# Building the one-hot matrix of an edge step with four VectorE comparisons instead of one

## What is computed

```python
Wh = (h @ W).reshape(N, HEADS, OUT_CH)                     # N = 6250, 4 heads x 64
e = einsum(Wh[edge_row], a_src) + einsum(Wh[edge_col], a_dst)
e = exp(leaky_relu(e) - max)
e_sum = segment_sum(e, edge_row)
alpha = e / (e_sum[edge_row] + 1e-15)
h_new = segment_sum(Wh[edge_col] * alpha, edge_row)        # a sum per target node
```

## Time and profile before

| | |
|---|---|
| median of 3 runs | 4566.98 us (4551.9 to 4567.17) |
| the profiled execution | 4563.81 us |
| its span, first to last instruction | 4561.9 us |
| busy: PE / DVE / ACT / POOL | 73% / 59% / 39% / 56% |
| stretch with the key side, 208 steps | 630 to 1939 us |
| stretch with the query side, 196 steps | 1939 to 3450 us |
| last stretch, 36 steps | 3450 to 3680 us |

### The profile page before, as it was taken

How to read it: one execution, slowest core, us unless ns; L and a number is a source line. 1 busy time by engine, 2 the same in 40 slices (tenths; PEclk the granted TensorE clock), 3 DMA queues, 4 the chain that set the end, 5 groups by cost and what they waited for, 6 DMA issues and landing times.

```text
span 4561.9 us, 90761 instructions
## 1 busy us (share of the span) xinstructions
PE 3309.0 (73%) x23188; PEld 2345.3 (51%) x23505; DVE 2688.7 (59%) x6015; ACT 1791.1 (39%) x4855; POOL 2546.9 (56%) x2454
## 2 busy tenths in 40 slices
PE   5888747767767777777777777777776545877895
PEld 2333324444444444456665666666564435665785
DVE  9888876657667666655555555555554463534222
ACT  3666422223323223244444444444443212543563
POOL 4566457767778867755565555555555613234223
PEclk8676668879989979889888989989897776988998
DMA  2222123333333323322222222222222232334344
GB/s 66 77 76 77 60 84 90 87 94 91 98 93 94 106 78 91 98 73 73 70 76 68 73 75 72 71 75 71 68 74 64 72 127 71 110 105 146 97 133 138
DMA packets 260611, 394.74 MB, mean 87 GB/s; under 512 B 71952, under 2 KB 195022, under 8 KB 260232
## 3 DMA queue, kind: packets, MB, share of 16 engines
q0 software_dynamic: 86704, 239.52, 18.9%
q1 hardware_dynamic: 150924, 132.95, 9.4%
q10 hardware_dynamic: 22860, 20.83, 1.6%
HBM read 308.82 MB, written 84.30 MB: 86 GB/s over the span
## 4 chain that ended last, share of the span: by engine, by line
PE 29%; issue 20%; DVE 13%; another core or an unknown queue 12%; DVEq 12%; ACT 7%; POOL 4%; ACTq 2%; DMA 1%; POOLq 0%; SPq 0%
PE bank L1935 6%; PE bank L1856 5%; DVEq L1445 4%; DVEq L1468 4%; PE bank L2123 3%; PE bank L2135 3%; DVEq L1444 3%; PE bank L1858 2%; PE bank L1969 2%; ACT away L1028 2%; DVE room L1438 1%; POOL room L805 1%; PE bank L1924 1%; DVE room L1464 1%
## 5 line engine op out<-in xcount | busy, mean ns | idle before, releaser
L805 POOL DMA_INDIRECT room<-table,room x1564 | 1804.0, 1153 | 1091.6 <-DVE room L1464 645.5
L1935 PE MATMUL bank<-room 128*128 128x260 f32 x3520 | 1020.7, 439 | 380.3 <-issue 208.0
L1935 PEld LDWEIGHTS bank<-room 128*128 128x128 f32 x3520 | 730.5, 218 | 512.0 <-issue 398.9
L1484 DVE TENSOR_TENSOR room<-room 128x1024 f32<-128x1024 f32 x392 | 481.2, 1228 | 533.0 <-issue 499.1
L1464 DVE TENSOR_TENSOR room<-room 128x1024 f32<-128x1024 f32 x440 | 537.0, 1220 | 389.7 <-ACT room L1037 268.4
L1028 ACT ACTIVATE away<-bank,minus_p 128x512 bf16<-128x512 f32 x440 | 301.7, 686 | 1084.7 <-remote 980.2
L1969 PE MATMUL bank<-ident,room 128*128 128x128 f32 x1764 | 262.1, 299 | 206.6 <-DVE room L1487 142.7
L1856 PE MATMUL bank<-room 128*128 128x264 f32 (+1 forms) x588 | 312.8, 673 | 65.8 <-issue 34.4
L1031 ACT ACTIVATE spare<-away,ones 128x512 bf16<-128x512 bf16 x440 | 317.6, 722 | 54.2
L1969 PEld LDWEIGHTS bank<-ident,room 128*128 128x128 f32 x1764 | 218.6, 154 | 197.1 <-issue 185.6
L1924 PE MATMUL bank<-rowt,spare 128*128 128x8 bf16 x7040 | 262.1, 167 | 73.2 <-issue 72.5
(11 more groups left out here) (313 smaller groups left out, 4793.0 us busy)
## 6 DMA issues: line engine op xcount, KB each, us to landing
room<-table,room POOLq DMA_INDIRECT x1564
kv_dram<-room SPq DMA_DIRECT2D x49, 324.0 KB, 2.2
room<-kv_dram SPq DMA_DIRECT2D x196, 81.0 KB
y_dram<-planes SPq DMA_DIRECT2D x119, 128.0 KB
room<-xs_dram ACTq DMA_DIRECT2D x110, 128.0 KB
q_dram<-room SPq DMA_DIRECT2D x49, 192.0 KB, 1.8
room<-q_dram SPq DMA_DIRECT2D x196, 48.0 KB
table<-room SPq DMA_DIRECT2D x49, 130.0 KB, 2.1
```

The lines of the kernel that those rows point to most:

```text
L805: pool.indirect_dma_start(G[:, k.slot, u, :], None, table, bass.IndirectOffsetOnAxis(ap=ixbuf[:, k.slot, u:u + 1].bitcast(I32), axis=0)).t ...
L1484: dve.tensor_tensor(f.rearrange("p h (d i) -> p h d i", i=MD), over(x, [[XD, 2], [0, h], [1, MD]]), over(x, [[XD, 2], [1, h], [1, MD]]), A ...
L1935: ins = pe.matmul(pbank[1 + h][:, 0:TW], OH[:, s, u, :], Gw[:, h, u, :], start=(u == 0), stop=(u == U - 1))
```

## The change

The one comparison of two inputs (`iota_f` repeated four times, and the four row numbers each repeated 128 times, 512 columns) becomes four comparisons of 128 columns, each with one row number per partition as a scalar operand. All four write their quarter of the same slot of `OH`; the semaphore is raised by the last.

```diff
             if k.after(4):
                 dve.wait_ge(agg_made, k.n - 3)
-            dve.tensor_tensor(OH[:, s, :, :], iota_f[:].unsqueeze(1).to_broadcast([P, U, P]),
-                              row_step[:, bass.ds(k.n, 1), :].rearrange("p a u -> p (a u)").unsqueeze(2).to_broadcast([P, U, P]),
-                              ALU.is_equal).then_inc(oh_done, 1)
+            for u in range(U):
+                ins = dve.tensor_scalar(OH[:, s, u, :], iota_f[:], row_step[:, bass.ds(k.n, 1), u:u + 1].rearrange("p a u -> p (a u)"), None, ALU.is_equal)
+            ins.then_inc(oh_done, 1)
```

## The result

| | before | after |
|---|---|---|
| median | 4559.44 us (4 runs, 4551.77 to 4567.17) | 4697.49 us (4 runs, 4687.35 to 4716.8) |
| the profiled execution's span | 4561.9 us | 4686.7 us |

The ratio is 1.0308, with a 95% interval from 1.0262 to 1.0353: the change costs 138 us. The forecast was 4650 us, 1.8% slower, so the sign and the mechanism came true and the sum of 88 us was 50 us too small. The two profiled executions lie 125 us apart; between them all of the misfit lies in the first stretch, as will be seen.

The account below looks back on a forecast made before the run. The prediction took VectorE's queue to bound the first stretch, and partly the second, with a TensorE-ScalarE circle. Terms 53 + 19 + 11 + 5 = 88 us gave 4652 from the profiled run, forecast as 4650 us; range 4575 to 4730 us.

Parts of the forecast that it names:

- The bound: VectorE's queue, handing over loads ahead of `features`, outlasts its datapath by 0.94 us in steps of the key side.
- The price of a pair: On VectorE's queue, one address computation with its instruction costs 0.15 us; three more cost 0.45 us per loop step.
- Who pays: Key side: three of four steps, less 18 waiting for ScalarE, pay 0.45 us each: 53 us.
- The knock-on: Steps where `weigh` waits for ScalarE were only taken off the paying ones: 18 on key side, 79 on query side.
- The second stretch: Query side: 38 us of queue delay, half counted because a later ScalarE wait may swallow it: 19 us.
- The last stretch: Last 32 loop steps: three of four pay 0.45 us of queue work, 11 us.
- The fixed-address steps: 40 steps outside loops: three bare instructions more, half of 0.24 us of comparison time counted each, 5 us.
- The datapath: VectorE's four comparisons take 0.84 us against 0.60; the 0.24 us more is hidden beside the queue in loop steps.
- GpSimd: Gathers waiting for `weigh` before reusing a place: nothing counted; at most 0.24 us in each of 440 steps, 106 us.
- Absorbed: Rival: TensorE, ScalarE and VectorE's circle sets the lap, ScalarE waits shrink; some 11 us, 4575 us, chance 0.15.
- Faster: Rival: comparisons cost 0.13 us each on the datapath, `weigh` ends 0.07 us earlier; at most 31 us gained, chance 0.05.
- Lock: Rival: each comparison waits 0.49 us for a GpSimd gather; 220 us, 4870 us; sign, comparisons over 0.5 us; chance 0.07.

Follow-up runs that it names:

- five increments: Kernel before, plus five increments of an idle semaphore on VectorE's queue behind the comparison of each loop step: 4211.51 us against 4081.43, ratio 1.0315.
- fixed-place kernel: Changed kernel, its four comparisons reading row numbers from fixed places, without address work: 4087.09 us against 4081.43 for the kernel before; on another chip 4475.7 against 4470.54.
- eight comparisons: Kernel with four comparisons reading fixed places, plus four more per loop step into a spare place: 4636.74 us against 4461.63 for the kernel before, ratio 1.0392.

## Why the prediction was right, and where it fell short

- **The bound.** The queue of VectorE sets the steps of the first stretch: right. Take the address work away and the loss is gone (165 against 5 us on one chip), queue work alone makes such a loss (130 and 300 us), and less of it was a gain of 185 us on the first chip. The reading rested on one idle time with the releaser "issue", its count, and the loads in the chain of waits.
- **The price of a pair.** 0.15 us forecast, 0.13 measured; three are 0.39 us, inside the bounds of 0.36 and 0.48. A usual step became 0.385 us longer.
- **Who pays.** This is the term that was mis-sized. The forecast let "three of four" steps pay, after taking off the 18 that wait for ScalarE, since one step of the pattern looked as if it had 0.39 us of slack. The usual lap became 1.54 us longer, which is 4 x 0.385: all four pay, the lap with that step too. 176 x 0.385 makes 68 us, where 53 stood. With five increments the first chip gave 70 of 82 in this stretch and with the second five all of it.
- **The knock-on.** The forecast let a wait for ScalarE only take something off the sum. It also adds: 39 us in the first stretch of the profiled pair, 53 and 57 on the second and third chips, since, as I read the traces, steps that had just escaped the late ScalarE ran into it (the third chip's number is against the kernel with fixed row numbers). For this reading: on the first chip, which has no late signals, the same kind of delay added nothing beyond the usual steps (3 us against 6). No run removed the late signals on a chip that has them, so it is argued and not shown. With 39 us of the 41 by which the first stretch exceeds its 53, this is the larger part of the misfit; full payment gives 14, and the 12 that the rest became shorter go the other way. The upper end of the range had a term for later gathers and for full payment and none for this, so that the result lies inside is partly luck.
- **The second stretch.** 19 us forecast, 16 in the profiled pair, 29 on the second chip and 50 on the third; there the half that a wait for ScalarE would swallow was a guess between ends, and the runs lie on both sides of it, so the near hit is luck. On the first chip the five increments cost 58 of 89 there, although `weigh` waits for ScalarE only 19 us from 600 to 3700 us. So a late ScalarE is not all that swallows; what else does is open.
- **The last stretch**: 11 us forecast, 9 measured. **The fixed-address steps**: 5 us forecast for 40 steps. The fixed-place kernel costs 5 and 6 us in all 440 steps, so this term was hardly more.
- **The datapath.** 0.84 us forecast for the four, 0.79 measured; its cover held, as the fixed-place kernels show on two chips. The sentence on what a lost cover costs (400 x 0.24 us, linear) is too simple: eight comparisons show a loss that comes from late steps.
- **GpSimd.** The forecast counted nothing. It also says that the range takes in 106 us from later gathers; it does not, since its upper end holds 24 us of that. The runs do not separate such a term.
- **The rivals.** *Absorbed* fell with the first stretch. *Faster* fell twice: a comparison starts every 0.20 us, not 0.13, and `weigh` is later. *Lock* fell with the mean of 295 ns, where it had 0.49 us more for each, and with the kernel without address work, which has the same four comparisons among the gathers and loses 6 us; a single comparison of 515 ns just passes the sign of 0.5 us that was set for it.

What stays open: why the signal from TensorE to ScalarE comes late on three of the four occasions and never on the first chip, and what in the third slot of passes 3 and 4 meets it. It is not ScalarE alone: TensorE hands over slowly in the same microseconds, and on the third chip VectorE's `scores` (L1455) wait 102 us without a named releaser, in 22 steps, where the same kernel on the first chip has no such wait. No run here took it apart. The 12 us by which the rest of the first stretch became shorter in the profiled pair aren't explained either; the second chip's pair shows 7, the third's none.

## What to carry to other kernels

An instruction inside a hardware loop whose address depends on the counter costs the queue 0.13 us before the datapath sees it, 0.10 of it for the address, and a step whose first real work waits for "issue" pays for each of them; splitting one instruction into four is then dear although its datapath work is hidden. Before counting such a delay once, look for steps that already wait for another engine elsewhere in the pattern: a uniform delay can move others into the same wait, and what came on top was more than half as much again here. And a gain by relieving one queue needs a second chip: what gave 4.6% on one cost 1.1% on another, where a second bound stood close and the late signals grew.

## What the runs showed of the hardware

- The same kernel takes 4081 us on one chip and 4462, 4471 and 4559 us in the other three comparisons, a spread of 12%, and each is steady in itself (the seven runs on the second lie between 4440 and 4489 us). None of the three chips of the experiments was used on a second occasion, so the runs do not say that it is the chip and not something else about the occasion. The kernel with fixed row numbers was profiled on two of them, 4079 and 4475 us. Its VectorE is busy equally long on both (2773 and 2775 us). On the fast chip ScalarE starts L1028 0.43 us after L1911's start when it waits for it, and on the other it waits up to 10.9 us with no releaser in the trace. The granted clock differs too: in the second stretch it is 1.00 on the fast chip, the 2.4 GHz level throughout, and 0.94 on the other, in the first 0.90 and 0.88. Which follows from which is not shown.
- Register work on VectorE's queue: 0.13 us for an address and the instruction behind it, 0.093 us for an increment of a semaphore, and some 0.03 us for a bare comparison with a fixed address, an estimate: four of them take the place of one pair without a change (0.43 against 0.44 us), and four more add 0.12 us. A load of a table value with its address and bound takes far more; two loads of the changed kernel, 0.53 us each, with the work behind them:

```profile
1519.50 0.53 DVEq L1445
1520.06 0.19 DVEq L1445
1520.43 0.53 DVEq L1468
1520.99 0.19 DVEq L1468
```

  That is 0.93 us from one load to the next (1519.50 to 1520.43), as much as seven pairs.
- A comparison of 128 columns with one scalar operand takes 281 ns, and the next starts 0.20 us after it, while it still drains. The estimate from the errata table of the Trainium skill ("VectorE: DVE Perf Modes", section "The TRN2 errata — SBUF-src ops pay a fixed extra latency per instruction"), 0.51 us for four, stays below the 0.79 us that they took, as the row-based price of 0.84 had said.
